# Two-layer network on one core: expert outputs combined before the transpose, attention's input steps re-ordered, its loops written out

## The reference, cut to what matters

```python
x = x + mamba(cond(x, ...), ...)                 # L0_attn
# L0_ffn: two experts a token
top_vals, top_idx = jax.lax.top_k(logits, 2)
routing = softmax(top_vals)
out = out + ye * sum(routing * (top_idx == e))[:, None]     # for every expert e
x = x + out
# L1_attn: input u = sigmoid(x) * base
k, v = split(u @ w_kv, 2)                        # 4 groups, 128 wide
scores = q @ k.T * 128 ** -0.5                   # 4 heads a group, causal
x = x + (softmax(scores) @ v) @ w_dense
# L1_ffn: input u = sigmoid(x) * base2
x = x + ((silu(u @ gate.T * gs) * (u @ up.T * us)) @ down.T) * ds
```

## Time and profile before

| | us |
|---|---|
| median of 3 runs | 2521.63 (2519.21 to 2541.95) |
| the profiled execution | 2520.18 |
| its span, first to last instruction | 2518.4 |
| mean granted TensorE clock | 0.974 |

### The profile page before, as it was taken

One profiled execution on the slowest core, in us unless ns is written; L12 is line 12 of the kernel. 1 busy time (PEld: TensorE's weight loads), 2 busy tenths in 40 slices (PEclk: granted clock), 3 DMA queues, 4 the chain that ended last, 5 costly groups with the idle time before them and its releaser, 6 DMA issues.

```text
span 2518.4 us, 33213 instructions
## 1 busy us (share of the span) xinstructions
PE 2231.3 (89%) x10427; PEld 1646.0 (65%) x10427; DVE 1861.7 (74%) x2830; ACT 1001.7 (40%) x2075; POOL 679.7 (27%) x544
## 2 busy tenths in 40 slices
PE   0789989989897899789879999999999988999998
PEld 0344444444445778677668888878888876788886
DVE  8989898998978765676545667778777785666665
ACT  3243342442342444555334444444444444222222
POOL 5434434334331533444411012122112210000000
PEclk9999999999999899999989999999999998999999
DMA  5001001001023532452331010010010101000001
GB/s 210 17 26 42 34 17 50 17 17 50 17 100 143 184 131 81 163 194 89 128 118 34 1 34 25 8 43 17 17 38 29 43 17 51 26 25 25 25 12 67
DMA packets 52812, 148.83 MB, mean 59 GB/s; under 512 B 5008, under 2 KB 5008, under 8 KB 48336
## 3 DMA queue, kind: packets, MB, share of 16 engines
q1 hardware_dynamic: 34144, 96.08, 10.8%
q10 hardware_dynamic: 12864, 32.81, 3.5%
q0 software_dynamic: 5680, 18.62, 2.5%
HBM read 113.14 MB, written 34.34 MB: 59 GB/s over the span
## 4 chain that ended last, share of the span: by engine, by line
PE 34%; issue 32%; POOL 11%; DVE 9%; POOLq 7%; ACT 3%; DMA 2%; ACTq 1%; DVEq 0%; another core or an unknown queue 0%; SPq 0%
PE bank L342 9%; PE bank L344 9%; PE bank L343 9%; POOLq L497 2%; PE bank L2347 2%; POOL g_v L505 2%; POOL g_v L498 2%; POOLq L520 1%; POOLq L523 1%; POOL g_s L519 1%; POOLq L509 1%; DVE rinv L1983 1%; PE bank L2398 1%; PE bank L2400 1%; POOL g_v L521 1%
## 5 line engine op out<-in xcount | busy, mean ns | idle before, releaser
L2222 PE MATMUL bank<-um,w_in 128*128 128x512 f32 x576 | 264.2, 613 | 5.6 <-DVE lm L1566 5.4
L2222 PEld LDWEIGHTS bank<-um,w_in 128*128 128x128 f32 x576 | 110.4, 197 | 137.0 <-issue 128.9
L342 PE MATMUL bank<-u_hi,aw_hi 128*128 (+1 forms) x384 | 158.3, 412 | 12.9 <-DVE u_lo L1963 9.1
L1186 ACT ACTIVATE probs<-bank,nmx 128x128 f32<-128x128 f32 (+3 forms) x256 | 131.6, 527 | 93.5 <-DVE nmx L1986 93.5
L1193 ACT ACTIVATE pt_hi<-bank 128x512 fp32r<-128x512 f32 (+1 forms) x192 | 94.0, 526 | 163.1 <-PE bank L2347 162.7
L344 PE MATMUL bank<-u_hi,aw_lo 128*128 (+1 forms) x384 | 151.9, 395 | 0.0
L343 PE MATMUL bank<-u_lo,aw_hi 128*128 (+1 forms) x384 | 151.5, 395 | 0.0
L452 DVE TENSOR_TENSOR_SCAN g_s<-decay,g_s 128x512 f32<-128x512 f32 x96 | 133.5, 1432 | 7.9 <-POOL g_v L498 7.9
L2398 PE MATMUL bank<-mw,bu_hi 128*128 (+1 forms) x312 | 127.9, 410 | 12.7 <-DVE mw L1850 7.3
L2001 DVE TENSOR_TENSOR pt_lo<-bank,pt_hi 128x512 fp32r<-128x512 f32 (+1 forms) x192 | 108.7, 593 | 39.1 <-ACT pt_hi L1193 37.6
L344 PE MATMUL bank<-u_hi,fw_lo 128*128 128x512 f32 x352 | 137.0, 389 | 0.0
(11 more groups left out here) (384 smaller groups left out, 6167.2 us busy)
## 6 DMA issues: line engine op xcount, KB each, us to landing
m_stage<-in_moe SPq DMA_DIRECT2D x21, 1024.0 KB, 6.7
y_slot<-m_o ACTq DMA_DIRECT2D x39, 256.0 KB
g_v<-in_fT SPq DMA_DIRECT2D x18, 512.0 KB, 3.6
gates<-g_v SPq DMA_DIRECT2D x18, 512.0 KB, 2.8
f_stage<-in_ffn SPq DMA_DIRECT2D x11, 768.0 KB, 4.2
u_g<-gates SPq DMA_DIRECT2D x8, 1024.0 KB, 10.7
aw_in<-in_att SPq DMA_DIRECT2D x4, 1280.0 KB
w_in<-in_w_in ACTq DMA_DIRECT2D x1, 4640.0 KB, 16.7
```

The lines of the kernel that those rows point to most:

```text
L342: nc.tensor.matmul(out, hi_w, hi_x, start=start, stop=False)
L1186: A(probs[:, h % 2, PR_AT[qb]:PR_AT[qb] + w], S_[bk][:, c0:c0 + w], ACT.Exp, bias=nmx[:, h % 2, qb:qb + 1], scale=SCALE, accum_out=rsum[:, ...
L2222: mm = M(dst[:], w_in[:, k, c0:c0 + P], um[:, k, :], start=(k == 0), stop=(k == KC - 1))
```

## The change

`w_diag` and `spread_weights` go. ScalarE scales the first gathered output in place (`scale_outputs`), VectorE multiplies the second with its weight and adds the first (`sum_outputs`), and TensorE transposes the sum, one transpose for each column chunk, in place of two matmuls. In iteration 0 VectorE's work of batch 1 stands ahead of `ctx_lo(0, 0)` and its gate and low part come earlier among the steps of head 1. The feed-forward inputs of batches 0 and 1 are cut in four steps: tanh stays where it was, gate, high and low part go to head 0 and 1 of the next iteration; batch 2's go into iteration 15. The loops over iterations become Python loops on the three engines, and their branches conditions of the source.

```diff
-            def spread_weights(b):
-                if b:
-                    act.wait_ge(cb_T, TB * b)
-                for a in range(b * TB, (b + 1) * TB):
-                    for k in range(2):
-                        A(w_diag[:, a % TB, k, :], ident[:], ACT.Copy, scale=we[:, k, a:a + 1]).then_inc(w_spread, 1)
+            def scale_outputs(b):
+                for tb in range(TB):
+                    a = b * TB + tb
+                    act.wait_ge(og_in[tb], 32 * (b + 1))
+                    A(og[:, tb, 0, :], og[:, tb, 0, :], ACT.Copy, scale=we[:, 0, a:a + 1]).then_inc(og_scaled, 1)
...
-            spread_weights(0)
             att_hi(1, 0)
+            scale_outputs(0)
             first_input()
-            spread_weights(1)
...
                 probs_exp(i, 1)
+                if mod == 6:
+                    if u == GROUPS - 2:
+                        input_hi(0, True)
+                if last:
+                    input_hi(1, True)
...
                 v_hi_copy(i)
+                if first:
+                    scale_outputs(1)
...
-                pt_hi_copy(i, 1)
+                if first:
+                    pt_hi_copy(i, 1, (0, 1))
+                    input_hi(1)
+                    pt_hi_copy(i, 1, (2,))
+                else:
+                    pt_hi_copy(i, 1)
                 probs_exp(i, 2)
-                if first:
-                    input_hi(1)
-                    spread_weights(2)
                 q_hi_copy(i, 3)
+                if last:
+                    gated_input(2, True)
...
                 probs_exp(i, 3)
+                if last:
+                    input_hi(2, True)
...
                     q_hi_copy(i + 1, 1)
+                if first:
+                    scale_outputs(2)
+                if mod == 1:
+                    scale_outputs(3)
                 if mod == 4:
                     att_hi(u + 2, 1)
                 pt_hi_copy(i, 3)
...
                 if first:
                     gated_input(2)
-                    spread_weights(3)
...
-                    with act.If(u == GROUPS - 2):
+                    if u == GROUPS - 2:
                         gated_input(mod - 5, True)
...
-            with act.Fori(0, GROUPS - 1) as u:
+            for u in range(GROUPS - 1):
...
-            gated_input(2, True)
...
             gated_input(3, True)
+            input_hi(3, True)
...
+            def sum_outputs(b, tb):
+                a = b * TB + tb
+                dve.wait_ge(og_scaled, a + 1)
+                first, second = og[:, tb, 0, :], og[:, tb, 1, :]
+                V.scalar_tensor_tensor(first, second, we[:, 1, a:a + 1], first, ALU.mult, ALU.add).then_inc(og_summed, 1)
...
             def batch_input(b):
+                sum_outputs(b, 0)
                 for tb in range(TB):
+                    if tb < TB - 1:
+                        sum_outputs(b, tb + 1)
                     combine(b, tb)
...
                 pt_lo_split(i, 0, (2,))
                 if mod in (1, 2):
                     gated_input(mod + 1)
+                if mod == 6:
+                    if u == GROUPS - 2:
+                        gated_input(0, True)
+                if last:
+                    gated_input(1, True)
                 if not first:
                     dense_add(i - 1, 0)
                 normalise(i, 1)
+                if mod == 6:
+                    if u == GROUPS - 2:
+                        input_lo(0, True)
+                if last:
+                    input_lo(1, True)
...
+                if first:
+                    batch_input(1)
                 ctx_lo(i, 0)
                 if first:
-                    batch_input(1)
+                    gated_input(1)
                 pt_lo_split(i, 1, (0, 1))
                 row_max(i, 2)
                 pt_lo_split(i, 1, (2,))
                 if first:
-                    gated_input(1)
+                    input_lo(1)
...
                 normalise(i, 2)
-                if first:
-                    input_lo(1)
+                if last:
+                    gated_input(2, True)
...
                 normalise(i, 3)
+                if last:
+                    input_lo(2, True)
...
-            with dve.Fori(0, GROUPS - 1) as u:
+            for u in range(GROUPS - 1):
...
-            gated_input(2, True)
...
             gated_input(3, True)
+            input_lo(3, True)
...
             def combine_T(b, tb):
-                pe.wait_ge(og_in[tb], 32 * (b + 1))
-                pe.wait_ge(w_spread, 2 * (a + 1))
+                pe.wait_ge(og_summed, a + 1)
                 if a >= 2:
                     pe.wait_ge(cb_done, a - 1)
                 for kc in range(KC):
                     o = slice(kc * P, (kc + 1) * P)
-                    for k in range(2):
-                        mm = M(TT_[tb % 2][:, o], og[:, tb, k, o], w_diag[:, tb, k, :], start=(k == 0), stop=(k == 1))
+                    mm = transposed(TT_[tb % 2][:, o], og[:, tb, 0, o])
...
-                        with pe.If(i < BATCH - 1):
+                        if i < BATCH - 1:
                             pe.wait_ge(u_split, i + (2 + IN_PARTS))
...
-                        with pe.If(i == 1):
+                        if i == 1:
                             batch_T(3)
...
-            with pe.Fori(1, NI - 1) as i:
+            for i in range(1, NI - 1):
                 att_pe(i, False, False)
```

More of the change, by code:

```diff
@@ L241, in network @@
                 cx_lo = sb("cx_lo", [P, HPG, T], F32R, s2)
-                w_diag = sb("w_diag", [P, TB, 2, P], F32, s2)
             with ExitStack() as s2:
@@ L297, in network @@
         og_in = [sem(f"og_in{i}") for i in range(TB)]
-        w_spread, cb_T, cb_done = sem("w_spread"), sem("cb_T"), sem("cb_done")
+        og_scaled, og_summed, cb_T, cb_done = sem("og_scaled"), sem("og_summed"), sem("cb_T"), sem("cb_done")
         a_staged, aw_hi_ready, aw_split = ([sem(f"{n}{i}") for i in range(3)] for n in ("a_staged", "aw_hi_ready", "aw_split"))
@@ L1119, in gated_input @@
                 A(u_in[:, :, tok(b % BATCH)], XT[:, :, tok(b % BATCH)], ACT.Tanh, scale=0.5).then_inc(x_tanh, 1)
-                if ffn:
-                    input_hi(b, ffn)
             def input_hi(b, ffn=False):
@@ L1188, in probs_exp, with pt_hi_copy @@
                       accum_out=rsum[:, h % 2, qb:qb + 1]).then_inc(exp_done, 1)
-            def pt_hi_copy(i, h):
-                for r, (bk, w, c0) in enumerate(T_GROUP):
+            def pt_hi_copy(i, h, groups=(0, 1, 2)):
+                for r in groups:
+                    bk, w, c0 = T_GROUP[r]
                     act.wait_ge(t_done, 3 * (HPG * i + h) + r + 1)
@@ L1954, in gated_input @@
                 V.scalar_tensor_tensor(u, u, 1.0, u_g[:, :, tok(b % BATCH)], ALU.add, ALU.mult).then_inc(u_ready, 1)
-                if ffn:
-                    input_lo(b, ffn)
             def input_lo(b, ffn=False):
@@ L2138, in att_dve @@
                     batch_input(3)
-                if mod in (5, 6):
-                    with dve.If(u == GROUPS - 2):
-                        gated_input(mod - 5, True)
             att_dve(0, "first")
```

## The result

Changed kernel: median 2495.89 us (2491.91 to 2509.96, 4 runs), beside it the kernel before 2529.94 (4 runs); ratio 0.9881, 95% interval 0.9833 to 0.9929. It is faster by 1.2%, and the time lies 8.9 us above the forecast of 2487, inside its range. The profiled execution took 2494.08 us, its span 2491.2; before it was 2520.18 and 2518.4. So the span got 27.2 us shorter, 1.1%, where the steps of the forecast add up to 34.2. Executions fall into two groups about 20 us apart, the slower one with a mean granted clock about 0.01 lower (here two of four before, 2538.25 and 2541.95, and one of four after, 2509.96), so a median depends on how many of each it holds, most of all in u1_loops and u2_ffn_order with five of ten in the slower group, while every profiled execution is of the faster.

The account below looks back on a forecast made before the run. TensorE was taken as the bound wherever it is fed, leaving its idle or repeated work to win. Terms summed to 34.2 us off the profiled 2520.18, hence 2486, stated as 2487 for the median; range 2476 to 2502.

Parts of the forecast that it names:

- batch 0: Combining expert outputs between the experts' end and the first key projection: gain 1.5 us, bounds loss 1 to gain 2.4.
- batch 1 stage: Adding batch 1's expert outputs: 4.8 us against 8.65, as two sums run before TensorE arrives; gain 3.9 us.
- chain to keys(1): Iteration 0, resumption to the transposes behind keys(1): 12.9 us instead of 22.89 by the new order; gain 10.0.
- batch 2 and 3, with the late pt_hi: Stages of batches 2 and 3: 7.1 us each, including 1.6 for scalings delaying pt_hi; gains 2.3 and 1.3.
- behind batch 2, and clock: Transposes after batch 2 start earlier without spread_weights(3), gain 2.6; lower clock behind sparse batch stages, loss 1.1 us.
- loops: Loops written out: ScalarE's stalls at two loop returns go; gain 0.9 us, bounds loss 5 to gain 2.
- feed-forward: heads of 14, 15: Heads of iterations 14 and 15: waits of 5.51 and 4.23 us and slow stretches behind them go; gain 13.5.
- feed-forward: last iteration: Batch 2's feed-forward steps moved into the last iteration: 2.3 us on the path, a 1.61 wait gone; net 0.7 lost.
- B: Clock rival: sparse stages lower TensorE's clock in all four batches, keys slow longer; 7 us more, 2494; chance 0.13.
- C: Work moved, not removed: scalings and last iteration's steps exposed at full price; 9.4 us less gain, 2496.5; chance 0.16.
- D: Iteration 0's stalls shrink beyond keys(1) and batches gain their upper bounds; 8 us more gain, 2479; chance 0.06.
- E: Written-out instruction stream isn't fetched in time: 18 to 28 packets, 18 costing TensorE 67 us, 2553; chance 0.05.

Follow-up runs that it names:

- u1_loops: Changed kernel with its loops over iterations as hardware loops again on TensorE, ScalarE and VectorE; 2502.41 us, ratio 0.992 to the kernel before.
- u2_ffn_order: Changed kernel with the feed-forward input steps of batches 0, 1 and 2 back where they stood before; 2516.56 us, ratio 0.9955 to the kernel before.
- u3: Changed kernel with iteration 0 in its old order on ScalarE and VectorE, combining as changed; 2503.39 us, ratio 0.9898 to the kernel before.
- v1: Changed kernel with GpSimd's four products of the last expert gate pair moved to VectorE ahead of the sums; 2493.49 us, ratio 0.9851 to the kernel before.
- u5: Changed kernel with diagonal weights and two matmuls a chunk again for batch 0 alone; 2490.36 us.
- w2: Changed kernel with GpSimd products added beside batch 2's sums, each reading two different tiles and waiting for the one before; 2492.03 us.
- u4: Changed kernel with diagonal weights and two matmuls a chunk again in all four batches; 2495.66 us, ratio 0.9898 to the kernel before.
- v2: Changed kernel with sums of batches 1 to 3 ahead of their stages, scalings of 2 and 3 one head earlier; 2481.31 us, ratio 0.9818 to before.
- v4: Changed kernel with 29 filler matmuls on TensorE in front of its waits in iteration 15; 2488.48 us, ratio 0.9828 to the kernel before.
- x1: Changed kernel with three pairs of 128x320 GpSimd products added beside batch 2's sums, each reading two different tiles; 2491.72 us.
- w1: Changed kernel with batch 0 on diagonal weights, later batches' sums and scalings earlier, and fillers in iteration 15; 2475.77 us, ratio 0.9781 to the kernel before.
- v3: Changed kernel with four 128x512 GpSimd products, each squaring a tile, added beside batch 2's sums; 2491.42 us.

## Why the prediction was right, and where its terms failed

Range and sign held; 34.2 us were summed and 27.2 came. Five terms came out above the forecast, by 2.4 us together, and the others 9.4 below it, so 2.4 us of error cancel by luck. Of the 7 us that are left, 2.6 are the experts' end and F, which differ between executions of one kernel and belong to no step. The terms (batches 2 and 3: the stages' 4.7 and 3.05 less the 1.7 and 1.4 by which the transposes before them came later; behind batch 2: from resumption to the stage of batch 3 51.60 us before, 51.93 after, of which 1.38 is counted with batch 3):

| step | forecast | measured |
|---|---|---|
| batch 0 | +1.5 | -1.7 (A) |
| batch 1 stage | +3.9 | +3.4 |
| chain to keys(1) | +10.0 | +10.2 |
| batch 2 and 3, with the late pt_hi | +2.3, +1.3 | +3.0, +1.7 |
| behind batch 2, and clock | +2.6, -1.1 | +1.05 |
| loops | +0.9 | +1.8 (G) |
| feed-forward: heads of 14, 15 | +13.5 | +13.7 (H) |
| feed-forward: last iteration | -0.7 | -3.1 (I) |
| experts' end; F; rest | 0 | -1.1; -1.5; -0.2 |

**Right.** The chain to keys(1) was followed instruction by instruction and came within 0.2 us, and u3 shows that it is the order that does it. The two heads came within 0.2, waits and slow clock together, and u2 brings both back. "Transposes 13 us behind the resumption" (12.65), "at most 5.5 us in each of batch stages 1 to 3" (5.35) and "dense(15, 3) without a wait" hold. "No pt_lo wait over 1 us" holds at the heads of iterations 14 and 15, the places of the earlier trace rows; inside iteration 15 three such waits stand, 2.18, 2.36 and 1.02 us, and the second was 1.07 before.

**Batch 0, the term that failed** (3.2 of the 7 us). The step "each priced like its addition, 0.69 us" took the duration of an operation that reads one tile from PSUM for one that reads two from SBUF, beside GpSimd. 0.75 us is right where GpSimd is idle, and up to 2.91 was taken where it is not. v1 shows the cause. It shows a second one too: with the sums fast 1.1 of the 3.2 us come back, and A is still 0.6 longer than before, since the gathers and, behind them, the scalings (0.72 us each, not 0.62) come last, the bound of the forecast that said "a loss of 1". The diagonals (u5, 2.0 us less) need no scaling and no sum after the gather.

The Trainium skill (SBUF — State Buffer, Who interferes with whom) says that a VectorE instruction with two SBUF inputs and a GpSimd instruction that reads SBUF exclude each other for the length of an instruction, and that the order of issue decides who waits. The trace agrees on the exclusion: 2.91 us for 0.75, and in w2 the product waits. On the order it agrees in part: the sum of 2.91 us started at 1248.26, ahead of the second product (1249.35), and was held through that one as well. A row that would have warned stood in the trace of before (last section).

**Batch 2.** The forecast says that half of 1.96 us may return, which is 0.98, and takes off 0.6; with 0.98 its term is 2.0 in place of 2.3, and 3.0 came.

**Last iteration** (2.4 us). The net of 0.7 lost was put together from steps alone; what was left out is the clock. TensorE waits 8.9 us in five places there (the four longest are shown), where it waited 9.2 in six before, so the waits as such did not grow. But it runs at a mean clock of 0.69 over the 25 us of row 7, and the kernel before at 0.86 in the same stretch (2114.38 to 2139.38). Over the whole of column I the mean clock is 0.81 in the changed kernel and 0.92 in the kernel before. At that same 0.92 the new order took 43.11 us (u4 and v2) and the old order 42.63 (before) and 43.82 (u2): at an equal clock the moved steps cost nothing that can be told. With the clock held at 1.00 the new order takes 41.2 (v4); the old order with fillers was not run. How much of it falls to one execution differs by 4 us: the ten profiles of the same instructions average 45.3, which would be -2.7 in place of -3.1. Two profiles have the old order, so whether the new order lowers the clock or these two were lucky stays open.

**Loops.** Worth 1.8 against 0.9: the two iterations in which ScalarE returns got 0.70 and 0.81 us shorter, not the 0.4 and 0.5 of TensorE's one wait at each; 0.2 more is spread over the iterations behind them.

**Rivals.** B: its price was wrong, its mechanism in part right. The clock did fall behind batch 2 (0.58 for 4.06 us); the last transposes of head 0 came 4.68 us behind the resumption there and 3.75 in v2, where it stayed up, so that fall cost 0.9 us, not 7. Behind the stage of batch 3, of the same transposes, it stayed at 1.00. Over the ten runs with stages like these (5.3 to 6.0 us) it fell to 0.58 to 0.64 behind batch 2 in seven, behind batch 3 in three (u1, u3, x1), and behind neither in u5; with diagonals in these stages (before, u4) or with stages of 3.5 us (v2, w1) it never did. In u2 it was 0.58 behind batch 1 as well, and C is 41.02 there for 41.04: the slack after batch 1 hides it, as the forecast says. The rule of the Trainium skill quoted with B (TensorE: Matmul & The Clock Gate, Part 4: PE-mode transpose) would fit the stages behind which the clock fell and not the others; TensorE is also idle for longer in them than with diagonals, and no run here separates the two. C: wrong for batches 2 and 3, which gained 4.7 instead of nothing; the last iteration lost 2.4 of the 5.8 us that C takes off the feed-forward part, and without the "waits over 2 us more". D: no. E: refuted by u1; the fetch queue moved 26 packets more, within the estimated 18 to 28, and they cost TensorE nothing that the cuts show.

## What to carry to other kernels

Take the duration of an added operation from a row with the same sources (SBUF or PSUM), and look what GpSimd does in that window: VectorE's sums of two SBUF tiles and GpSimd's products held each other up here, so keep them apart in time; v2, which puts the sums of the later batches into VectorE's gaps, got them at 0.75 us each. Where an order of steps is changed, follow it instruction by instruction from the rows: at the two places where that was done in full it came within 0.2 us here. When an engine that sets the end must wait in many short pieces, price the clock behind them too, and try fillers: 29 unused matmuls were worth 2 to 6 us here.

## What the runs showed that was not expected

The same exclusion stands in front of a wait of TensorE of 1.8 to 3.7 us in iteration 3 of every kernel here, in code that the change doesn't touch. Timeline of the changed kernel, VectorE's scaling of four columns beside GpSimd's aw_lo, and TensorE:

```profile
1466.50 5.65 POOL L415 TENSOR_TENSOR aw_lo<-aw_in,aw_hi 128x2560 fp32r<-128x2560 f32 x1
...
1468.50 3.67 DVE L2001 TENSOR_SCALAR nmx<-rinv 128x4 f32<-128x4 f32 x1
...
1472.64 0.77 PE L341 MATMUL bank<-pt_hi,v_hi 128*128 128x512 f32 x1 [3.06 <-DVE pt_lo L2016]
```

The 128x4 operation lasts 0.17 us at 58 of its 64 places in this profile; here it ends at 1472.17, with GpSimd's instruction at 1472.15, though it has one SBUF source only. At the five others it stands beside an aw_lo of GpSimd too, and lasts 2.33 us (iterations 7 and 11, with waits of TensorE of 1.72) and 0.85 us (5, 9 and 13). The Trainium skill (SBUF — State Buffer, Who interferes with whom) has tensor_scalar among the operations that can take both ports; this row agrees. In the kernel before the same operation lasted 3.67 us at 1484.81. TensorE waits 3.06 us for it, and its clock behind that was 0.69 over 5.4 us in this profile and 1.00 in v3's, where the wait was 1.79. This is the spread of column F: 53.6 with the short wait (v3, w2, x1), 54.9 with 3.07 and the clock at 1.00 (v2, w1), 56.2 to 56.5 with a wait like it and the clock at about 0.7 (changed kernel, u1, v4), 58.2 with 3.73 and 0.53 (v1). The nearest cure, aw_lo cut in pieces, was not tried.

An instruction of GpSimd that only issues a gather is held too: 2.54 us in the kernel before, 2.63 in the changed kernel and 3.58 in v1 for 0.95, each beside VectorE's aw_lo.
